# Attention and routing phase of a fused four-block model: another order of TensorE's groups

## Chip, cores and metric

The kernel runs on one core of a Trainium2 chip. The metric is the device time of one execution in microseconds (us), the median of several runs. A profile of one execution, taken apart from those runs, gives the rows shown here.

## What is computed

Four layers, each a cross attention and a feed-forward block, on `x` of 16 x 256 x 256 in float32. Only the first three steps lie in phase A, which the change touches:

```python
x = x + tanh(g_xattn[0]) * _L0_xattn_ref(ctx, _layernorm(x), mask, ...)   # 16 heads of 64, keys: 256 context + 256 latent tokens
x = x + tanh(g_ffn[0]) * _L0_ffn_ref(_layernorm(x), ...)                  # attention over 256 tokens, 16 heads of 16, gated heads
x = x + tanh(g_xattn[1]) * _L1_xattn_ref(_layernorm(x), ctx, W_out, b_out, 16)   # 16 heads of 16, keys = values = context
...
```

In the wide attention (`_L0_xattn_ref`) `sim = q @ k.T`, masked, softmax over 512 keys, times `v`, times `Wout`, layer norm. Phase A also computes the router logits of the next step (an argmax over 32 experts).

## The kernel before

Everything is written by hand for five engines that meet at semaphores. Phase A has one loop over rounds `i = -1 .. B+1` (B = 16). Round `i` works on three batches at once: the wide attention of batch `i`, the narrow attention "f" (the gated one) of batch `f = i-1` with its end, and the narrow attention "c" of batch `c0 = i-2`. A round has eight **pairs** `u` of wide heads, and a pair has five **places** `p = 5u .. 5u+4`; `beside(i, p)` holds the narrow work of a place. Each engine runs the same loop over its own part, in program order.

TensorE's (PE's) groups, with the letters used from here on, the line of the profile and the part of the 128 x 128 array that a matmul of theirs uses (rows*columns as the trace prints it):

| letter | function | line | array | what |
|---|---|---|---|---|
| S | `scores(w,u,t)` | L543 | 64*128 | scores of two wide heads, for query tile t = 0 or 1 |
| K, Q | `keys`, `pair_queries` | L522, L531 | 128*128 | keys, queries of the **next** pair |
| V | `values` | L551 | 128*128 | values of this pair |
| PT | `weights_by_key` | L561 | 128*128 | transposes of softmax weights, four per pair |
| AV | `pair_values` | L573 | 128*64 | weights times values of the pair **before** |
| wo | `wide_out` | L584 | 128*128 | output projection |
| bq, bk | `by_query`, `by_key` | L689, L703 | 32*128 | narrow scores, four groups g = 0..3 each, once by query and once by key |
| vo | `values_out` | L718 | 128*32 | narrow weights times values |
| tq, tt, to, cT | `turn_queries`, `turn_tiles`, `turn_out`, `c_keys` | L666, L612, L731, L658 | 128*128 | transposes |
| fq, fk | `f_rows`, `f_keys` | L625, L633 | 128*128 | narrow projections |
| gate, elog, cnt | `f_gate`, `e_logits`, `e_count` | L641, L747, L219/L220 | 128*128 | gate logits, router logits, expert counts |

"S1" is S for t = 1; "bq3" is bq with g = 3. The part of the array is called the **mode** below.

PSUM is shared by order. The wide work rotates through 3 banks (`w_order`, a list that names every wide group in PE's order): a group may start when the group three places before it in that list has been taken out by its reader. The narrow scores rotate through 2 slots of two banks (`n_order`), and one bq or bk fills both. Readers: VectorE (DVE) masks each S (`mask_scores`, L1080, one per head), reduces each half of a bq to its maxima (`maxima`, L1155), and copies half of the PTs (L1090). ScalarE (ACT) copies K, Q, V and AV (L884, L889, L894, L901), takes the exponentials of the wide weights in SBUF (`exps`, L877) and of each half of a bk out of PSUM (L934), and copies the transposed queries of a tq (L924), which the next bq or bk reads. GpSimd scales the wide weights.

Of the kernel before, what the change touches and what calls it, by code (L numbers as in the profile page):

```python
# [89 lines left out]
PAIRS = HEADS // 2  # L90
# [4 lines left out]
def build(nc, a, out, B, stages):  # L95
# [5 lines left out]
    with top:  # L101
# [130 lines left out]
        def on(b):  # L232
            return 0 <= b < B
# [7 lines left out]
        if "A" in stages:  # L241
            with ExitStack() as ph:
# [58 lines left out]
                def filled(i, p):  # L301

                    return fill.get((i, p), [])

                w_order = []
                for i in range(-1, B + 2):
                    for u in range(PAIRS):
                        nw, nu = pair_after(i, u)
                        bw, bu = pair_before(i, u)
                        w_order += [("S", i, u, 0, j) for j in range(2)] * on(i) + [("K", nw, nu)] * on(nw)  # L310
                        w_order += [("wo", i - 1)] * (u == 1 and on(i - 1)) + filled(i, 5 * u)
                        w_order += [("S", i, u, 1, j) for j in range(2)] * on(i) + [("Q", nw, nu)] * on(nw) + filled(i, 5 * u + 1)
                        w_order += [("V", i, u)] * on(i)
                        w_order += [("lT", i + 1)] * (u == 6 and on(i + 1)) + filled(i, 5 * u + 2)
                        w_order += [("AV", bw, bu)] * on(bw)
# [8 lines left out]
                for i in range(B + 2):  # L324
                    f, c0 = i - 1, i - 2
# [5 lines left out]
                with Stage() as ctx:  # L331
# [168 lines left out]
                    def _(pe):  # L500
# [250 lines left out]
                        def e_count(b):  # L751
                            pe.wait_ge(e_chosen, b + 1)
                            route_count(pe, rb, b, vbank).then_inc(vr.full(("rk", b)), 1)

                        def beside(i, p):
                            f, c0 = i - 1, i - 2
                            if on(c0):
                                if p == 1:
                                    queries_again("c", c0)
                                if 2 <= p <= 5:  # L760
                                    by_key("c", c0, p - 2)
                                if 3 <= p <= 6:
# [8 lines left out]
                                if p == 18:  # L771
                                    e_turn(c0)
                                if p == 20:
                                    e_logits(c0)
                                if p == 23:
                                    e_count(c0)
                            if on(f):
                                if p == 5:
                                    wide_out(f, 0)
                                    wide_out(f, 1)  # L780
                                if p == 11:
                                    f_turn(f)
                                if p == 12:
                                    f_rows(("fq", f), f, fq)
                                if p == 13:
                                    f_keys(f)
                                if p == 14:
                                    f_rows(("fv", f), f, fv)
# [8 lines left out]
                                if 24 <= p <= 27:  # L797
                                    values_out("f", f, p - 24)
                                if p == 28:
# [11 lines left out]
                                if 36 <= p <= 38:  # L811
                                    by_query("c", f, p - 36)
                            if on(i + 1):
                                if p == 32:
                                    features(("lT", i + 1), i + 1, 0)
                                if p == 33:
                                    features(("xT", i + 1), i + 1, 2)

                        pe.wait_ge(made, 2)
                        for i in range(-1, B + 2):  # L820
# [3 lines left out]
                            for u in range(PAIRS):  # L824
                                nw, nu = pair_after(i, u)
# [2 lines left out]
                                    scores(i, u, 0)  # L828
                                if u == 0 and on(i - 2):
                                    by_query("c", i - 2, 3)  # L830
                                if on(nw):
                                    keys(nw, nu)
                                beside(i, 5 * u)
                                shared(i, 5 * u)
                                if on(i):
                                    scores(i, u, 1)
                                if u == 4 and on(i - 1):
                                    by_query("f", i - 1, 3)
                                if on(nw):
                                    pair_queries(nw, nu)  # L840
                                beside(i, 5 * u + 1)
                                shared(i, 5 * u + 1)
                                if on(i):
                                    values(i, u)
                                beside(i, 5 * u + 2)
                                shared(i, 5 * u + 2)
                                if on(bw):
                                    pair_values(bw, bu)
# [12 lines left out]
                    def _(act):  # L861
# [150 lines left out]
                        for i in range(-1, B + 2):  # L1012
                            for u in range(PAIRS):
                                nw, nu = pair_after(i, u)
                                bw, bu = pair_before(i, u)
                                if on(nw):
# [4 lines left out]
                                shared_tanh(i, 5 * u)  # L1021
                                if on(nw):
                                    pair_queries(nw, nu)
                                if u == 3 and on(i - 1):
                                    turn_queries(("f", "Q", i - 1))
                                if on(i):
                                    exps(i, u, 1)
                                beside(i, 5 * u + 1)
                                shared_tanh(i, 5 * u + 1)
                                if on(i):  # L1030
                                    values(i, u)
                                beside(i, 5 * u + 2)
                                shared_tanh(i, 5 * u + 2)
                                if on(bw):
                                    pair_values(bw, bu)
# [13 lines left out]
                    def _(dve):  # L1049
# [167 lines left out]
                        def beside(i, p):  # L1217
# [6 lines left out]
                                if p == 9:  # L1224
                                    c_add(c0)
                            if on(f):
                                if p == 5:
                                    wide_take(f)
                                if p == 7:
                                    wide_ask(f)  # L1230
# [1644 lines left out]
```

## Time and profile before

| what | value |
|---|---|
| median of 3 runs | 4381.85 us (4377.96 to 4382.2) |
| the profiled execution: its own time | 4407.42 us |
| its span from first to last instruction | 4405.7 us |
| PE busy | 4046.3 us, 92% of the span |
| DVE, ACT, GpSimd busy | 53%, 40%, 21% |
| one steady round of phase A | 146.90 us |

Phase A is the first 2300 us or so of the span. PE is the engine to read: it is busy nearly all the time there, and its idle time has a releaser beside it, the engine whose work ended the wait. In the timeline a row is a run of equal instructions; the difference between the starts of two rows of PE is what the first one costs, waits included. The "us" column of a matmul row is a modelled end and overlaps the next row.

### The profile page before, as it was taken

The page shows a single profiled execution, that of the slowest core. Times are in us where ns is not written, and L with a number is a line of the kernel's source. Part 1 is how long each engine was busy: PE and PEld are TensorE (multiplying, and loading weights), DVE is VectorE, ACT ScalarE, POOL GpSimd, SP SyncE. Part 2 cuts the span into 40 slices and gives each one's busy share as a digit, 9 for nine tenths or more (in the row PEclk, how much of TensorE's full clock was granted, in tenths as well). Part 3 has the DMA queues.
Part 4 walks back from the last instruction along what each step waited for, and adds up shares of the span by engine and source line. Part 5 has one row for each costly group of instructions (what it writes and reads, how often), then busy time and mean ns, then how long its engine had stood idle before and what let it go on. Part 6 is the DMA issues. An engine that isn't in the chain of part 4 may idle for free. (4 is left out here: it accounts for less than half of the span.)

```text
span 4405.7 us, 78115 instructions
## 1 busy us (share of the span) xinstructions
PE 4046.3 (92%) x29168; PEld 2823.8 (64%) x29168; DVE 2319.0 (53%) x7158; ACT 1776.4 (40%) x3733; POOL 945.1 (21%) x1115
## 2 busy tenths in 40 slices
PE   7999999999999999999999899988899998679986
PEld 4666666666666666666665599956666665448853
DVE  4555655565556555655554422135666665474434
ACT  4445544554455445554542111112444444213310
POOL 2221222122212221222120011110111100015556
PEclk9999999999999999999999999999999999889998
DMA  3000000000000000000000289920100100029944
GB/s 112 3 3 6 8 8 4 6 8 8 4 6 8 8 4 6 8 7 5 4 30 15 77 284 332 335 92 13 34 20 20 32 18 13 17 96 326 325 143 131
DMA packets 136623, 284.25 MB, mean 65 GB/s; under 512 B 19968, under 2 KB 90176, under 8 KB 127680
## 3 DMA queue, kind: packets, MB, share of 16 engines
q1 hardware_dynamic: 84944, 200.03, 13.2%
q0 software_dynamic: 18336, 50.09, 3.8%
q10 hardware_dynamic: 32976, 29.13, 1.9%
q8 instruction: 243, 3.98, 0.4%
q14 instruction: 124, 1.02, 0.1%
HBM read 229.12 MB, written 50.07 MB: 63 GB/s over the span
## 5 line engine op out<-in xcount | busy, mean ns | idle before, releaser
L459 POOL TENSOR_SCALAR a_wide_p<-a_wide_p,a_w_inv 128x512 f32<-128x512 f32 x512 | 354.8, 705 | 1427.0 <-DVE a_w_inv L1085 1427.0
L877 ACT ACTIVATE a_wide_p<-a_wide_p,a_row_min 128x512 f32<-128x512 f32 x512 | 363.5, 713 | 6.1 <-DVE a_row_min L1080 2.8
L1080 DVE CUSTOM_DVE_ANT_0 a_wide_p<-ring,a_neg_keys 128x512 f32<-128x512 f32 x434 | 285.1, 688 | 124.5 <-PE ring L543 124.2
L1155 DVE TENSOR_REDUCE a_q_pad<-ring 128x4 f32<-128x1024 f32 x256 | 301.4, 1220 | 90.0 <-PE ring L689 88.1
L543 PE MATMUL ring<-a_qk 64*128 64x512 f32 x868 | 288.5, 640 | 19.7 <-DVE a_wide_pt L1090 15.5
L934 ACT ACTIVATE a_probs<-ring 128x1024 f32<-128x1024 f32 x256 | 250.5, 1018 | 76.4 <-PE ring L703 76.4
L1574 PE MATMUL ring<-b_xgt,b_we 128*128 128x128 f32 x2016 | 235.5, 275 | 0.5 <-DVE b_xgt L1737 0.5
L1574 PEld LDWEIGHTS ring<-b_xgt,b_we 128*128 128x128 f32 x2016 | 230.2, 192 | 0.8 <-DVE b_xgt L1737 0.7
L2640 DVE CUSTOM_DVE_ANT_0 c_junk<-ring,c_neg_mask 128x256 f32<-128x256 f32 x512 | 181.4, 420 | 90.0 <-PE ring L2170 90.0
L573 PE MATMUL ring<-a_wide_pt,a_v 128*64 128x256 f32 x1792 | 219.5, 387 | 0.0
L551 PEld LDWEIGHTS ring<-shared_w,a_kv_t 128*128 128x128 f32 x1568 | 185.0, 192 | 20.0 <-issue 12.3
L551 PE MATMUL ring<-shared_w,a_kv_t 128*128 128x128 f32 x1568 | 195.6, 278 | 1.7
L1503 POOL DMA_INDIRECT d_xg<-d_rows,d_token_idx x159 | 150.3, 945 | 183.9 <-PE ring L1563 82.7
L884 ACT ACTIVATE a_qk<-acc 128x512 f32<-128x512 f32 x82 | 49.0, 597 | 310.5 <-PE acc L522 310.5
L689 PE MATMUL ring<-a_k_t,a_q_t 32*128 32x256 f32 x2048 | 146.6, 399 | 27.7 <-DVE a_q_pad L1155 22.6
L573 PEld LDWEIGHTS ring<-a_wide_pt,a_v 128*64 128x64 f32 x1792 | 119.3, 137 | 81.2 <-issue 21.2
L703 PE MATMUL ring<-a_q_t,a_k_t 32*128 32x256 f32 x2048 | 147.6, 401 | 23.5 <-ACT a_probs L934 18.2
L561 PE MATMUL ring<-ident,a_wide_p 128*128 128x128 f32 x1208 | 164.0, 275 | 5.5 <-ACT a_kv_t L868 4.9
L1747 DVE TENSOR_TENSOR b_hid<-b_sil,ring 128x512 f32<-128x512 f32 x63 | 43.3, 687 | 238.2 <-ACT b_sil L1635 238.2
L1574 PE MATMUL ring<-d_xgt,d_we 128*128 128x128 f32 x1272 | 168.2, 275 | 0.5 <-DVE d_xgt L1737 0.5
L522 PE MATMUL acc<-a_kv_t,shared_w 128*128 128x512 f32 x328 | 164.4, 624 | 1.2 <-ACT a_kv_t L868 1.2
L2441 ACT ACTIVATE c_probs<-ring 128x1024 f32<-128x1024 f32 x128 | 125.7, 1023 | 94.9 <-PE ring L2186 94.9
(461 smaller groups left out, 8421.8 us busy)
## 6 DMA issues: line engine op xcount, KB each, us to landing
b_we<-in_experts SPq DMA_DIRECT2D x63, 1536.0 KB
d_we<-in_experts SPq DMA_DIRECT2D x159, 256.0 KB
d_results<-d_yb ACTq DMA_DIRECT2D x159, 128.0 KB
b_results<-b_yb ACTq DMA_DIRECT2D x63, 128.0 KB
a_cb<-in_ctx SPq DMA_DIRECT2D x16, 256.0 KB, 2.8
b_turned<-a_heads_t SPq DMA_DIRECT2D x16, 256.0 KB
b_rows<-a_heads SPq DMA_DIRECT2D x16, 256.0 KB
shared_x<-b_turned SPq DMA_DIRECT2D x8, 512.0 KB, 5.4
```

Of the source, the lines that this page charges most:

```text
L459: ins = pool.tensor_scalar(wide_p[:, h % 4, t, :], wide_p[:, h % 4, t, :], w_inv[:, t, h:h + 1], 1.0, ALU.mult, ALU.mult)
L522: ins = pe.matmul(wbank(name), wkv[:, c, u * P:(u + 1) * P], kv_t[w % 2][:, c, :], start=(c == 0), stop=(c == C - 1))
L543: pe.matmul(wbank(name), qk[u % 2][64 * j:64 * j + 64, t * P:(t + 1) * P], qk[u % 2][64 * j:64 * j + 64, 256:768], start=True, stop=True). ...
L551: ins = pe.matmul(wbank(name)[:, P * i:P * i + P], kv_t[w % 2][:, c, i * P:(i + 1) * P], wkv[:, c, 1024 + u * P:1024 + (u + 1) * P], start ...
L561: ins = pe.transpose(wbank(name)[:, P * k:P * k + P], wide_p[:, (2 * u + h) % 4, t, k * P:(k + 1) * P], ident[:])
L573: ins = pe.matmul(wbank(name)[64 * h:64 * h + 64, 0:256], v4[u % 2][:, k, 64 * h:64 * h + 64], wide_pt[:, h, k, :], start=(k == 0), stop=( ...
L877: ins = act.activation(wide_p[:, h % 4, t, :], wide_p[:, h % 4, t, :], ACT.Exp, scale=-1.0, bias=row_min[:, h, t:t + 1], accum_out=row_sum ...
L934: act.activation(probs[:, i % 4, :, :, :].rearrange("p j k n -> p (j k n)"), nslot(name), ACT.Exp, scale=HD ** -0.5 if k == "c" else 1.0). ...
L1080: dve.tensor_tensor_reduce(wide_p[:, h % 4, t, :], wbank(name), neg_keys[w % 2][:], -0.125, 3.0e38, ALU.add, ALU.min, row_min[:, h, t:t + ...
L1155: dve.tensor_reduce(q_pad[:, :, 2 * i:2 * i + 2, HD].rearrange("p t h -> p h t"), s, AX.X, ALU.max, negate=True).then_inc(nr.taken(name), 1)
L1574: ins = pe.matmul(ring[:, rg.slot(("gu", u)), UP * j + P * i:UP * j + P * i + P], we[:, u % WB, w0:w0 + P], xgt[:, u % 2, c, :], start=(c ...
L2640: ins = dve.tensor_tensor_reduce(junk[:, 4 * (i % 2) + 2 * j + t, :], s[:, j, t, :], neg_mask[:, t, :], -1.0, 3.0e38, ALU.add, ALU.min, q_ ...
```

## The change

It rearranges PE's groups within a pair and moves no work to another engine. Two tables of pair numbers decide it. In the pairs of `late` (0, 1, 4, 5) K of the next pair stands behind S1 in place of in front of it. In the pairs of `near` (1, 2, 5, 6) AV of the pair before stands right behind S1, and Q and V come after it. `w_order` (the rotation) and ACT's program follow the same tables. Single groups move too: bq3 of "f" goes ahead of S1 in pair 4, bq0 of "c" goes ahead of Q in pair 7, wo from place 5 to 6, elog from place 20 to 19, two of the vo stand together at place 27. DVE's program changes in two places: `maxima("f", f, 3)` moves from place 21 to 20, and `wide_take` from 5 to 6. No instruction is added or dropped.

```diff
+                late = (0, 1, 4, 5)
+                near = (1, 2, 5, 6)
...
-                                if p == 20:
+                                if p == 19:
                                     e_logits(c0)
...
-                                if p == 5:
+                                if p == 6:
                                     wide_out(f, 0)
...
-                                if on(nw):
+                                if u == 4 and on(i - 1):
+                                    by_query("f", i - 1, 3)
+                                if u not in late and on(nw):
                                     keys(nw, nu)
                                 beside(i, 5 * u)
                                 shared(i, 5 * u)
                                 if on(i):
                                     scores(i, u, 1)
-                                if u == 4 and on(i - 1):
-                                    by_query("f", i - 1, 3)
+                                if u in near:
+                                    if on(bw):
+                                        pair_values(bw, bu)
+                                    beside(i, 5 * u + 1)
+                                    shared(i, 5 * u + 1)
+                                if u == PAIRS - 1 and on(i - 1):
+                                    by_query("c", i - 1, 0)
+                                if u in late and on(nw):
+                                    keys(nw, nu)
                                 if on(nw):
                                     pair_queries(nw, nu)
...
-                                if p == 21:
+                                if p == 20:
                                     maxima("f", f, 3)
```

**PE, pairs 3 and 4 of a steady round**, from the second bq on. Before (rows of S1 and of the PTs that name `ring` or `acc` are the same group in another bank):

```order
L689 MATMUL ring<-a_k_t,a_q_t 128x256 x8
L561 MATMUL acc<-ident,a_wide_p 128x128 x4
...
L689 MATMUL ring<-a_k_t,a_q_t 128x256 x8
L543 MATMUL ring<-a_qk 128x512 x2
L522 MATMUL acc<-a_kv_t,shared_w 128x512 x2
L747 MATMUL acc<-b_route_w,a_heads_t 128x32 x4
L543 MATMUL ring<-a_qk 128x512 x2
L689 MATMUL ring<-a_k_t,a_q_t 128x256 x8
L531 MATMUL acc<-a_kv_t,shared_x 128x256 x2
```

After, the same stretch (lines are 7 higher):

```order
L696 MATMUL ring<-a_k_t,a_q_t 128x256 x8
L619 MATMUL acc<-ident,a_heads 128x128 x4
L568 MATMUL acc<-ident,a_wide_p 128x128 x4
...
L754 MATMUL acc<-b_route_w,a_heads_t 128x32 x4
L696 MATMUL ring<-a_k_t,a_q_t 128x256 x8
L550 MATMUL ring<-a_qk 128x512 x2
L696 MATMUL ring<-a_k_t,a_q_t 128x256 x8
L550 MATMUL acc<-a_qk 128x512
L550 MATMUL ring<-a_qk 128x512
L529 MATMUL ring<-a_kv_t,shared_w 128x512 x2
L538 MATMUL acc<-a_kv_t,shared_x 128x256 x2
```

Between bq2 and bq3 there stood S, K, elog and S1; now S alone stands there, and elog is ahead of bq2.

**DVE at the same place**: before, the masks of S and S1 stand together around the router logits, and the maxima of bq3 follow.

```order
L1155 TENSOR_REDUCE a_q_pad<-ring 128x2x2 x2
L1080 ISA a_wide_p,a_row_min<-ring,a_neg_keys 128x512
L1080 ISA a_row_min 128x1
L1080 ISA a_wide_p,a_row_min<-ring,a_neg_keys 128x512
L1080 ISA a_row_min 128x1
L186 COPY b_logits<-acc 128x64
L1080 ISA a_wide_p,a_row_min<-ring,a_neg_keys 128x512
...
L1155 TENSOR_REDUCE a_q_pad<-ring 128x2x2 x2
```

After:

```order
L1198 TENSOR_REDUCE a_q_pad<-ring 128x2x2 x2
L1123 ISA a_wide_p,a_row_min<-ring,a_neg_keys 128x512
L1123 ISA a_row_min 128x1
L1123 ISA a_wide_p,a_row_min<-ring,a_neg_keys 128x512
L1123 ISA a_row_min 128x1
L1198 TENSOR_REDUCE a_q_pad<-ring 128x2x2 x2
L186 COPY b_logits<-acc 128x64
L1123 ISA a_wide_p,a_row_min<-acc,a_neg_keys 128x512
```

The maxima of bq3 have moved ahead of the mask of S1.

The whole round as letters, read from the two orders, with | where the mode changes and - where it stays:

```
before                                              after
0 S|bq|K|S|Q-tq-V|bk|AV|bk|vo|PT4|bk|vo|            S|bq|S|K-Q-tq-V|bk|AV|bk|vo|PT4|bk|vo|
1 S|K|bk|vo|wo|S|Q|vo|V-to|AV|tt-PT4-proj|          S|bk|vo|S|AV|vo|wo-K-Q-to-V-tt-PT4-proj|
2 S|K|S|Q-tt-V-fq|AV|fk-PT4-fv|                     S|K|S|AV|tt-Q-fq-V-fk-PT4-fv|
3 S|K|S|Q-tq-V|bq|AV|tt|bq|PT4|bq|                  S|K|S|Q-tq-V|bq|AV|bq|tt-PT4-elog|bq|
4 S|K-elog|S|bq|Q-V-tq|AV|cnt|bk|PT4|bk|vo|         S|bq|S|K-Q-V-tq|AV|bk|cnt-PT4|bk|vo|
5 S|K|bk|vo|S|Q|bk|vo|V|vo|AV|to-PT4-tt|            S|bk|vo|S|AV|bk|K-Q|vo-vo|V-to-PT4-tt|
6 S|K-gate|S|Q-proj-V-cT-lT|AV|xT-PT4|              S|K-gate|S|AV|proj-Q-cT-lT-V-xT-PT4|
7 S|K-tq|S|Q|bq|V|bq|AV|PT2|bq|PT2|                 S|K-tq|S|bq|Q-V|bq|AV|PT2|bq|PT2|
```

Over all of phase A the mode changes 1270 times in PE's order before and 1048 times after; in a steady round (2 to 14) 78 and 64 times, counting the change to the next round's S.

## Rows read from the trace of the kernel before

**Rows 1.** Windows, a steady round: us, busy PE, PEld, DVE, ACT, POOL, clock, DMA share, GB/s

```profile
983.90:1130.80 146.90, 141.61 (x1078) 94.22 (x1078) 84.55 (x231) 75.36 (x158) 32.61 (x40) 1.00 0.02 7
```

**Rows 2.** Timeline, PE: the four PT of pair 3, two of them in the second row

```profile
1059.70 0.66 PE L561 MATMUL acc<-ident,a_wide_p 128*128 128x128 f32 x4
1060.20 1.04 PE L561 MATMUL ring<-ident,a_wide_p 128*128 128x128 f32 x8
1061.07 0.63 PE L561 MATMUL acc<-ident,a_wide_p 128*128 128x128 f32 x4
```

**Rows 3.** Timeline, PE: one K and two V, each with the row that follows it

```profile
1029.07 1.98 PE L522 MATMUL acc<-a_kv_t,shared_w 128*128 128x512 f32 x4
1030.99 1.13 PE L543 MATMUL ring<-a_qk 64*128 64x512 f32 x4
...
1018.14 2.05 PE L551 MATMUL ring<-shared_w,a_kv_t 128*128 128x128 f32 x16
1020.02 1.04 PE L731 MATMUL ring<-ident,a_o_t 128*128 128x128 f32 x8
...
1106.10 1.95 PE L551 MATMUL ring<-shared_w,a_kv_t 128*128 128x128 f32 x16
1107.88 1.04 PE L658 MATMUL ring<-ident,a_v_pad 128*128 128x128 f32 x8
```

**Rows 4.** Timeline, PE, pairs 3 and 4, from bq1 to bk0

```profile
1058.63 1.15 PE L689 MATMUL ring<-a_k_t,a_q_t 32*128 32x256 f32 x16
...
1062.30 1.15 PE L689 MATMUL ring<-a_k_t,a_q_t 32*128 32x256 f32 x16 [0.60 <-DVE a_q_pad L1155]
1063.38 1.13 PE L543 MATMUL ring<-a_qk 64*128 64x512 f32 x4
1064.44 1.98 PE L522 MATMUL acc<-a_kv_t,shared_w 128*128 128x512 f32 x4
1066.26 0.97 PE L747 MATMUL acc<-b_route_w,a_heads_t 128*128 128x32 f32 x8
1067.19 1.13 PE L543 MATMUL ring<-a_qk 64*128 64x512 f32 x4
1068.25 1.15 PE L689 MATMUL ring<-a_k_t,a_q_t 32*128 32x256 f32 x16
...
1073.32 1.95 PE L573 MATMUL ring<-a_wide_pt,a_v 128*64 128x256 f32 x16
1075.20 0.19 PE L219 MATMUL acc<-b_pairs,earlier 128*128 128x32 bf16 x1
...
1075.39 1.15 PE L703 MATMUL ring<-a_q_t,a_k_t 32*128 32x256 f32 x16
```

**Rows 5.** Timeline, DVE: maxima of bq2, then the first mask of S

```profile
1063.47 2.36 DVE L1155 TENSOR_REDUCE a_q_pad<-ring 128x4 f32<-128x1024 f32 x2
1065.74 0.68 DVE L1080 CUSTOM_DVE_ANT_0 a_wide_p<-ring,a_neg_keys 128x512 f32<-128x512 f32 x1
```

**Rows 6.** Timeline, pair 0: DVE's maxima of bq3; PE's Q, tq and bk0

```profile
986.56 2.35 DVE L1155 TENSOR_REDUCE a_q_pad<-ring 128x4 f32<-128x1024 f32 x2
...
989.03 1.13 PE L531 MATMUL ring<-a_kv_t,shared_x 128*128 128x256 f32 x4
990.00 1.04 PE L666 MATMUL ring<-ident,a_q_pad 128*128 128x128 f32 x8
...
993.11 1.15 PE L703 MATMUL ring<-a_q_t,a_k_t 32*128 32x256 f32 x16 [0.29 <-ACT a_q_t L924]
```

**Rows 7.** Timeline, PE: pair 2's S and fq

```profile
1028.02 1.13 PE L543 MATMUL ring<-a_qk 64*128 64x512 f32 x4 [0.93 <-DVE a_wide_pt L1090]
...
1035.81 1.97 PE L625 MATMUL acc<-a_fq,a_x_t 128*128 128x256 f32 x8 [0.41 <-ACT a_x_t L920]
```

**Rows 8.** Timeline, pair 7: PE's Q, bq0 and bq1

```profile
1119.33 1.13 PE L531 MATMUL ring<-a_kv_t,shared_x 128*128 128x256 f32 x4
1120.56 1.15 PE L689 MATMUL ring<-a_k_t,a_q_t 32*128 32x256 f32 x16
...
1124.23 1.15 PE L689 MATMUL ring<-a_k_t,a_q_t 32*128 32x256 f32 x16 [0.55 <-DVE a_q_pad L1155]
```

More of the change, by code:

```diff
@@ L309, in build @@
                         bw, bu = pair_before(i, u)
-                        w_order += [("S", i, u, 0, j) for j in range(2)] * on(i) + [("K", nw, nu)] * on(nw)
-                        w_order += [("wo", i - 1)] * (u == 1 and on(i - 1)) + filled(i, 5 * u)
-                        w_order += [("S", i, u, 1, j) for j in range(2)] * on(i) + [("Q", nw, nu)] * on(nw) + filled(i, 5 * u + 1)
+                        w_order += [("S", i, u, 0, j) for j in range(2)] * on(i)
+                        w_order += [("K", nw, nu)] * (u not in late and on(nw)) + filled(i, 5 * u)
+                        w_order += [("S", i, u, 1, j) for j in range(2)] * on(i)
+                        w_order += [("AV", bw, bu)] * (u in near and on(bw))
+                        w_order += ([("wo", i - 1)] * (u == 1 and on(i - 1)) + filled(i, 5 * u + 1)) * (u in near)
+                        w_order += [("K", nw, nu)] * (u in late and on(nw)) + [("Q", nw, nu)] * on(nw)
+                        w_order += filled(i, 5 * u + 1) * (u not in near)
+                        w_order += ([("lT", i + 1)] * (u == 6 and on(i + 1)) + filled(i, 5 * u + 2)) * (u in near)
                         w_order += [("V", i, u)] * on(i)
-                        w_order += [("lT", i + 1)] * (u == 6 and on(i + 1)) + filled(i, 5 * u + 2)
-                        w_order += [("AV", bw, bu)] * on(bw)
+                        w_order += (filled(i, 5 * u + 2) + [("AV", bw, bu)] * on(bw)) * (u not in near)
                         w_order += [("xT", i + 1)] * (u == 6 and on(i + 1)) + filled(i, 5 * u + 3)
@@ L796, in beside @@
                                     by_key("f", f, p - 23)
-                                if 24 <= p <= 27:
+                                if p == 24 or p == 25:
                                     values_out("f", f, p - 24)
+                                if p == 27:
+                                    values_out("f", f, 2)
+                                    values_out("f", f, 3)
                                 if p == 28:
@@ L810, in beside @@
                                     queries("c", f)
-                                if 36 <= p <= 38:
+                                if 37 <= p <= 38:
                                     by_query("c", f, p - 36)
+                            if on(c0):
+                                if p == 18:
+                                    e_turn(c0)
+                                if p == 23:
+                                    e_count(c0)
                             if on(i + 1):
@@ L836, in _ @@
                                     scores(i, u, 1)
-                                if u == 4 and on(i - 1):
-                                    by_query("f", i - 1, 3)
+                                if u in near:
[7 more added lines that the diff above has]
+                                    keys(nw, nu)
                                 if on(nw):
                                     pair_queries(nw, nu)
[L841 to L848, printed above, removed]
+                                if u in near:
+                                    beside(i, 5 * u + 2)
+                                    shared(i, 5 * u + 2)
+                                    if on(i):
+                                        values(i, u)
+                                else:
+                                    beside(i, 5 * u + 1)
+                                    shared(i, 5 * u + 1)
+                                    if on(i):
+                                        values(i, u)
+                                    beside(i, 5 * u + 2)
+                                    shared(i, 5 * u + 2)
+                                    if on(bw):
+                                        pair_values(bw, bu)
                                 if u == PAIRS - 1 and on(i):
@@ L1015, in _ @@
                                 bw, bu = pair_before(i, u)
-                                if on(nw):
+                                if u not in late and on(nw):
                                     keys(nw, nu)
@@ L1021, in _ @@
                                 shared_tanh(i, 5 * u)
+                                if u in near:
+                                    if on(i):
+                                        exps(i, u, 1)
+                                    if u > 1 and on(bw):
+                                        pair_values(bw, bu)
+                                    beside(i, 5 * u + 1)
+                                    if u == 1 and on(bw):
+                                        pair_values(bw, bu)
+                                    shared_tanh(i, 5 * u + 1)
@@ L1022, in _ @@
+                                if u in late and on(nw):
+                                    keys(nw, nu)
                                 if on(nw):
                                     pair_queries(nw, nu)
[L1024 to L1035, printed above, removed]
+                                if u in near:
+                                    beside(i, 5 * u + 2)
+                                    shared_tanh(i, 5 * u + 2)
+                                    if on(i):
+                                        values(i, u)
+                                else:
+                                    if u == 3 and on(i - 1):
+                                        turn_queries(("f", "Q", i - 1))
+                                    if on(i):
+                                        exps(i, u, 1)
+                                    beside(i, 5 * u + 1)
+                                    shared_tanh(i, 5 * u + 1)
+                                    if on(i):
+                                        values(i, u)
+                                    beside(i, 5 * u + 2)
+                                    shared_tanh(i, 5 * u + 2)
+                                    if on(bw):
+                                        pair_values(bw, bu)
@@ L1226, in beside @@
                             if on(f):
-                                if p == 5:
+                                if p == 6:
                                     wide_take(f)
```

4 lines of the change are left out of this document (removed).

## The prediction

> **What bounds the kernel now.** I read the windows first, then the timeline of PE over one steady round, then DVE's and ACT's timeline beside its waits. A steady round takes 146.90 us and PE is busy for 141.61 of them, so PE idles 5.29; the granted clock is 1.00, the 2.4 GHz level, and plays no part; DVE (84.55) and ACT (75.36) have room on average [rows 1]. What counts is therefore PE's own cost per group, and the few places where the next group waits for a reader: narrow scores that wait for maxima (0.60 and 0.55 us), a bk that waits for ACT's copy of the turned queries (0.29), S of pair 2 behind a long DVE stretch (0.93), fq behind ACT (0.41) [rows 4, 6 to 8].
>
> **Price of a mode change.** Two parts show in start-to-start times. Leaving: K followed by S, another mode, takes 1.92 us; K followed by elog, the same mode, takes 1.82 [rows 3, 4]. The rows round 0.09 or so up and down, and I count 0.093. Entering: V behind vo takes 1.88, V behind a group of its own mode 1.78, both left without a change [rows 3]: 0.10 more. For K and Q, which in the kernel before always come from another mode, I take V's 0.10, because they load full weights just as V does; nothing shows them without it. Nothing shows 64*128 followed by 128*64 (S then AV) either; I take 0.09, a change like any other, and keep 0 and 0.2 as its ends, which is 4 places a round and +-0.4 us.
>
> The Trainium skill's page "TensorEngine Tiling (Array Packing)", Key Properties, says that a change of the tiling mode, not of the tile alone, drains the engine. The 0.09 us on leaving agree with it, and by that rule alone the change could only gain: 222 changes at 0.093 are 20.6 us, 4361.
>
> **What the removed changes are worth.** The order has 14 fewer changes in a steady round: 14 x 0.093 = 1.30 us. Groups that newly come from their own mode: Q in pairs 0, 1, 2, 4, 5, 6, K in pair 1, V in pairs 1 and 7, fk in pair 2; proj in pair 6 newly comes from another. Net 9 x 0.10 = 0.94, and a net 0.22 for four transposing groups, which cost 0.50 as the first after a change and 0.44 otherwise [rows 2]. Together **2.46 us a round** if no wait changes. V in pair 7 is in this sum.
>
> **What the new order makes wait.** I walked the round with the durations of the rows, each group starting at the later of PE's turn and the release of what it needs. From the rows: bq, bk 1.08 (1062.30 to 1063.38), S 1.06, elog 0.93 [rows 4]; Q 0.97, and 0.87 from its own mode; tq 0.87 before its own mode [rows 6]; V 1.78 [rows 3]; AV 1.88 (1073.32 to 1075.20) [rows 4]; PT 0.44 [rows 2].
>
> *Pairs 3 and 4* carry most of it. bq2 starts at 1062.30 and its maxima at 1063.47, 2.36 us for both halves [rows 4, 5]. bq3 fills the same two slots, so it can't start before bq2 + 1.17 + 2.36 + 0.15 = bq2 + 3.68. Before, S, K, elog and S1 (4.87 us) cover that, and bq3 starts 5.95 after bq2 [rows 4]. Now only S does. bq1 stays at 1058.63 (it waits for DVE in both); behind it come tt 0.49, four PT 1.75, 0.18 for the last PT (its bank is emptied by ACT, which now has the copy of tt first) and elog 0.93, so bq2 starts at 1063.06 in place of 1062.30. S ends 2.14 later, at 1065.20, and bq3 waits until 1066.74: **a new wait of 1.54 us**. S1 follows at 1067.81, K at 1068.87 and ends at 1070.69. Q needs the bank of S1's first half. DVE masks it late, because the maxima of bq3 now come first: 1066.74 + 1.17 + 2.3 for the maxima, 0.3 for the logits (my guess, for a small copy that waits for its own semaphore), 0.68 for the mask [rows 5], 0.1 to PE: 1071.28, **another wait of 0.6**. Then Q 0.87, V 1.78, tq 0.97, AV 1.88: bk0 at 1076.78 against 1075.39. After bk0 both orders hang on the same ACT exponentials. Net +1.40, the removed changes already inside.
>
> *Pair 0.* bq3 of "c" starts as before and its maxima begin at 986.56, 2.35 long [rows 6]. S1 now stands right behind bq3, but DVE reaches its mask only at 988.84, so Q, three places behind S1's first half, can start at 989.6 and not at 989.03. ACT then copies Q (0.1 earlier after its start, since Q is shorter), takes the exponentials of S1 and copies tq, in this order; so the copy ends 0.45 later, and bk0 moves from 993.11 to 993.56 [rows 6]. Net +0.46.
>
> *Pair 7.* bq0 of "c" now stands ahead of Q. In the old order Q is in front of it and bq0 still waits 0.17 (1119.33 to 1120.56, Q being 1.06) for ACT's copy of tq. That copy doesn't come earlier, so PE now waits from 1119.33 to 1120.56, does bq0, Q and V (1.08 + 0.97 + 1.88) and has bq1 at 1124.49 against 1124.23; the old wait of 0.55 there is gone [rows 8]. Net +0.26.
>
> *Pairs that gain.* Pair 1: five fewer changes bring the group `to` 0.37 earlier. DVE's stretch from there (divide heads, layer norm, both copies of PT) sets S of pair 2 at 1028.02 [rows 7], so it moves with it: -0.37. Pair 2: fq waits for ACT's copy of tt, which now stands behind the exponentials of S1 and the copy of AV, 0.3 later than before (1035.81 [rows 7]); what V and fk save just covers it: -0.09. Pair 5: -0.47 by changes, +0.2 for a bk and a vo that wait for ACT: -0.27. Pair 6: ACT's `features` set its end in both: -0.09.
>
> **Sum.** 1.40 + 0.46 + 0.26 - 0.37 - 0.09 - 0.27 - 0.09 = **+1.3 us a round**, the waits growing by 3.76 us and the changes giving 2.46. Rounds 2 to 14 are alike: 13 x 1.3 = +17. Rounds 0 and 1: with no narrow work between, S1 stands directly behind S in six pairs and waits 0.9 for the mask of S, three places before its second half; against that, pair 1 of round 1 has wo ahead of its long wait and gains 2. Together about 0. The last round and the tail: +0.5. Other phases aren't touched. **+17 us**: against the profiled execution's own 4407.42 it is 4424; that execution lies 25.6 above the median of the runs, and the median goes from 4381.85 to **4399**.
>
> **Rivals.** (a) *The waits only move and don't grow*: the changes' 2.46 us a round, with 222 x 0.093 = 20.6 on leaving and 17.7 on entering in all of phase A, come off whole: 4381.85 - 38 = 4344. For it: PE is the busiest engine, and DVE and ACT have over 60 us of slack a round [rows 1]. Against it: that slack isn't at bq3. A milder form ends on the faster side too: the wait ahead of bq3 in pair 4 is overlapped, because bq3 in fact starts when DVE has finished one half. It decides from a growth of waits under 2.46 a round; with bq3's 1.54 and half of the other losses away, the sum is -0.8 x 14 = -11: 4371. (b) *Even*: my +1.3 is a difference of 3.76 and 2.46, and 0.6 less leaves it within 8.8 us of before. This happens if entering costs K and Q more than V's 0.10, or if DVE gets to S1's masks 0.3 sooner at pairs 0 and 4: 4381 to 4390. (c) *Worse*: waits behind ACT's new order that I took as covered, above all AV's copy in pair 1, which by the code must wait for the whole of wo and holds ACT for 7 us, or the exponentials of S1 in pair 4, reach PE: another 1 us a round, 4413.
>
> The skill's same page, PSUM Bottleneck, says that row tiling speeds the matmuls up but not the emptying of PSUM. The rows agree: 1.08 us on PE fill what takes DVE 2.36 [rows 4, 5]. It speaks for my forecast: groups of one mode side by side bring narrow scores closer together than DVE can empty them.
>
> **How the numbers follow.** A measurement of this kernel can tell 0.2% (8.8 us) from nothing. Slower as forecast, (c) with it: 0.62. Even: 0.19. Faster, whole or mild: 0.19. The range takes in (c) at the top (4418) and the milder form of (a) at the bottom (4366), and leaves the full gain out.
>
> **What would show it.** In the changed kernel's round: length 148.2 us and idle time of PE near 9 us in place of 5.3; mode changes cheaper by Q at 0.87 behind K; a wait of 1.5 us at bq of pair 4 released by the maxima, one of 0.6 at Q of pairs 4 and 0 released by the mask, one of 1.2 at bq0 of pair 7 released by ACT; the 0.60 at bq2 of pair 3 and the 0.55 at bq1 of pair 7 gone; S of pair 2 still behind DVE, now for 1.3 us. Wrong if the wait at bq3 is under 0.5 us, or if the round is under 146.

## The result and the profile after

| | before | after |
|---|---|---|
| median of 5 runs each | 4381.85 us | 4400.27 us (4395.28 to 4414.67) |
| ratio | | 1.0048, 95% interval 1.0037 to 1.0060 |
| a steady round | 146.90 us | 148.05 us |

The change makes the kernel 18.4 us slower. A ratio here and below, with its interval, is estimated from the executions of both kernels; it isn't the quotient of the two medians, which is 1.0042 here. The profiled executions took 4407.42 and 4414.67 us, both longer than any of the other executions of their kernel, and their spans (4405.7 and 4412.9 us) differ by less than the medians, so I compare rounds. In the page of after, PE is busy for less time than the 4046.3 us of before, and yet the kernel is slower:

```profile
span 4412.9 us, 78115 instructions
PE 4023.8 (91%) x29168; PEld 2835.4 (64%) x29168; DVE 2329.2 (53%) x7158; ACT 1770.5 (40%) x3733; POOL 946.1 (21%) x1115
```

The same steady round by windows (columns as in [rows 1]):

```profile
990.20:1138.25 148.05, 139.75 (x1076) 94.42 (x1077) 84.89 (x231) 74.76 (x158) 32.62 (x40) 1.00 0.02 6
```

Against [rows 1] PE's busy time fell by 1.86 us and its idle time rose from 5.29 to 8.30, by 3.01; the difference is the 1.15 us by which the round grew. (The idle time beside a row is less than the real wait, since the end of a matmul row is modelled; where sizes matter below, they are taken from starts.) The clock is 1.00, the 2.4 GHz level, as before. The view of PE's waits in this round says who is waited for (total, times, longest):

```profile
PE ring L696 <- DVE a_q_pad L1198: 2.2, 2, 1.5
PE ring L696 <- ACT a_q_t L950: 1.2, 1, 1.2
PE ring L550 <- DVE a_wide_pt L1133: 1.1, 1, 1.1
...
PE acc L632 <- ACT a_x_t L946: 0.6, 1, 0.6
PE ring L538 <- DVE a_row_min L1123: 0.3, 1, 0.3
...
PE acc L538 <- DVE a_row_min L1123: 0.3, 1, 0.3
```

Before, all the bq waited 1.1 us in the round for their maxima, and no Q for a mask. PE's timeline shows the places. Pairs 3 and 4 (compare [rows 4]), from bq1 to Q:

```profile
1065.05 1.15 PE L696 MATMUL ring<-a_k_t,a_q_t 32*128 32x256 f32 x16 [0.73 <-DVE a_q_pad L1198]
...
1068.45 0.98 PE L754 MATMUL acc<-b_route_w,a_heads_t 128*128 128x32 f32 x8
1069.36 1.15 PE L696 MATMUL ring<-a_k_t,a_q_t 32*128 32x256 f32 x16
1070.43 1.13 PE L550 MATMUL ring<-a_qk 64*128 64x512 f32 x4
1073.04 1.15 PE L696 MATMUL ring<-a_k_t,a_q_t 32*128 32x256 f32 x16 [1.48 <-DVE a_q_pad L1198]
...
1075.17 1.98 PE L529 MATMUL ring<-a_kv_t,shared_w 128*128 128x512 f32 x4
1077.49 1.13 PE L538 MATMUL acc<-a_kv_t,shared_x 128*128 128x256 f32 x4 [0.33 <-DVE a_row_min L1123]
```

bq3 stands one S behind bq2 and waits. DVE's timeline at that place (compare [rows 5]) shows for what, and why Q waits too, three groups after bq3:

```profile
1070.54 2.36 DVE L1198 TENSOR_REDUCE a_q_pad<-ring 128x4 f32<-128x1024 f32 x2 [0.77 <-PE ring L696]
1072.81 0.68 DVE L1123 CUSTOM_DVE_ANT_0 a_wide_p<-ring,a_neg_keys 128x512 f32<-128x512 f32 x1
...
1074.21 2.36 DVE L1198 TENSOR_REDUCE a_q_pad<-ring 128x4 f32<-128x1024 f32 x2
1076.48 0.21 DVE L186 COPY b_logits<-acc 128x64 f32<-128x64 f32 x1
1076.73 0.69 DVE L1123 CUSTOM_DVE_ANT_0 a_wide_p<-acc,a_neg_keys 128x512 f32<-128x512 f32 x1
```

The maxima of bq2 end at 1072.90 and bq3 starts at 1073.04. The mask of S1's first head ends at 1077.42 behind the maxima of bq3, and Q starts at 1077.49.

The other places in PE's timeline (compare [rows 6 to 8]): pair 0's Q and bk0, S of pair 2, fq, and bq0, Q, V, bq1 of pair 7:

```profile
995.90 1.13 PE L538 MATMUL ring<-a_kv_t,shared_x 128*128 128x256 f32 x4 [0.35 <-DVE a_row_min L1123]
...
999.91 1.15 PE L710 MATMUL ring<-a_q_t,a_k_t 32*128 32x256 f32 x16 [0.22 <-ACT a_q_t L950]
...
1034.44 1.13 PE L550 MATMUL ring<-a_qk 64*128 64x512 f32 x4 [1.12 <-DVE a_wide_pt L1133]
...
1042.50 1.97 PE L632 MATMUL acc<-a_fq,a_x_t 128*128 128x256 f32 x8 [0.63 <-ACT a_x_t L946]
...
1127.78 1.15 PE L696 MATMUL ring<-a_k_t,a_q_t 32*128 32x256 f32 x16 [1.16 <-ACT a_q_t L950]
1128.86 1.13 PE L538 MATMUL ring<-a_kv_t,shared_x 128*128 128x256 f32 x4
1129.82 1.95 PE L558 MATMUL acc<-shared_w,a_kv_t 128*128 128x128 f32 x16
1131.70 1.15 PE L696 MATMUL ring<-a_k_t,a_q_t 32*128 32x256 f32 x16
```

The distances between the first S of successive pairs, taken from the timelines of both traces, give what each pair cost (us, after less before):

| pair | forecast | measured |
|---|---|---|
| 0 | +0.46 | +0.47 |
| 1 | -0.37 | -0.37 |
| 2 | -0.09 | -0.02 |
| 3 and 4 | +1.40 | +1.28 |
| 5 | -0.27 | -0.37 |
| 6 | -0.09 | -0.09 |
| 7 | +0.26 | +0.25 |
| round | +1.3 | +1.15 |

### The profile page after: what moved, and what is told of

It is laid out like the page before. It is cut to its first block and busy times, and to the rows that moved or that the text cites. A ratio compares the mean times of both kernels' runs of the same rounds, so it can differ in the third digit from the quotient of the medians.

```text
span 4412.9 us, 78115 instructions
## 1 busy us (share of the span) xinstructions
PE 4023.8 (91%) x29168; PEld 2835.4 (64%) x29168; DVE 2329.2 (53%) x7158; ACT 1770.5 (40%) x3733; POOL 946.1 (21%) x1115
## 5 line engine op out<-in xcount | busy, mean ns | idle before, releaser
L1123 DVE CUSTOM_DVE_ANT_0 a_wide_p<-ring,a_neg_keys 128x512 f32<-128x512 f32 x387 | 256.1, 687 | 100.3 <-PE ring L550 99.9
L580 PE MATMUL ring<-a_wide_pt,a_v 128*64 128x256 f32 x1520 | 186.7, 388 | 0.0
L696 PEld LDWEIGHTS ring<-a_k_t,a_q_t 32*128 32x128 f32 x2048 | 95.9, 184 | 113.4 <-issue 108.0
L558 PE MATMUL ring<-shared_w,a_kv_t 128*128 128x128 f32 x1328 | 164.8, 277 | 1.7
L558 PEld LDWEIGHTS ring<-shared_w,a_kv_t 128*128 128x128 f32 x1328 | 157.5, 192 | 13.5 <-issue 6.5
L1133 DVE COPY a_wide_pt<-acc 128x512 f32<-128x512 f32 x127 | 87.5, 689 | 129.8 <-PE acc L568 129.8
```

What stands on the lines that cost most here:

```text
L558: ins = pe.matmul(wbank(name)[:, P * i:P * i + P], kv_t[w % 2][:, c, i * P:(i + 1) * P], wkv[:, c, 1024 + u * P:1024 + (u + 1) * P], start ...
L580: ins = pe.matmul(wbank(name)[64 * h:64 * h + 64, 0:256], v4[u % 2][:, k, 64 * h:64 * h + 64], wide_pt[:, h, k, :], start=(k == 0), stop=( ...
L696: ins = pe.matmul(nslot(name)[:, n:n + 256], q_t[SLOT * r:SLOT * r + SLOT, g, t * P:(t + 1) * P], k_t[SLOT * r:SLOT * r + SLOT, g, :], sta ...
L1123: dve.tensor_tensor_reduce(wide_p[:, h % 4, t, :], wbank(name), neg_keys[w % 2][:], -0.125, 3.0e38, ALU.add, ALU.min, row_min[:, h, t:t + ...
```

## The experiments

**The theory, called "local waits" below.** Each pair's entry in the table hangs on its own edit, so edits can be undone one by one and their rounds add up; what is lost in pairs 3 and 4 is DVE's time to empty the narrow scores. The rivals are named in each expectation. What follows phase A is the same program in all kernels and yet takes 1892 to 1939 us in the twelve traces, so the round decides where times don't. A "ratio" is against the kernel before on the same chip. The first four kernels ran on one chip, where the kernel before took 4383.85 us.

**1. Pairs 3 and 4 put back.** After, with

```diff
-                late = (0, 1, 4, 5)
+                late = (0, 1, 5)
...
-                                if u == 4 and on(i - 1):
-                                    by_query("f", i - 1, 3)
...
+                                if u == 4 and on(i - 1):
+                                    by_query("f", i - 1, 3)
...
-                                if p == 20:
+                                if p == 21:
```

The second pair of lines stands behind S1; the last is `maxima("f", f, 3)`; tt, elog and cnt are back too.

> The changed kernel with pairs 3 and 4 as before: K ahead of S1 in pair 4, bq3 behind S1, elog and cnt at their old places, the maxima of bq3 at place 21. Local waits (my theory): the round of 148.05 us loses the 1.28 us that pairs 3 and 4 gained, so 146.8, and the median comes back to that of before within 0.1% (4382). Rival, the loss is spread over the round by ACT's new order and the changed rotation: less than half of it comes back, round above 147.4, median 4390 or more.

Windows of its steady round:

```profile
983.40:1130.20 146.80, 140.11 (x1076) 94.66 (x1077) 84.39 (x231) 74.87 (x158) 32.62 (x40) 1.00 0.02 6
```

The round is 146.80, 1.25 under the 148.05 of after; the median is 4382.36, ratio 1.0006 (0.9996 to 1.0016). These two pairs are worth more than the whole loss of 1.15 a round.

**2. Pairs 3 and 4 alone.** Before, with only the edits that kernel 1 takes back (and `late = (4,)`, `near = ()`).

> The kernel before with the new pairs 3 and 4 alone. Local waits: round 146.90 + 1.28 = 148.2 us, median 4400, though 3 mode changes a round fewer. Rival, loss spread over the round: under half of that, round 147.5 or less, median under 4391.

Windows of its steady round:

```profile
991.20:1139.40 148.20, 141.28 (x1076) 94.05 (x1077) 85.08 (x231) 75.22 (x158) 32.60 (x40) 1.00 0.02 6
```

PE's timeline, bq3 and Q of pair 4:

```profile
1073.99 1.15 PE L696 MATMUL ring<-a_k_t,a_q_t 32*128 32x256 f32 x16 [1.48 <-DVE a_q_pad L1193]
...
1078.43 1.13 PE L538 MATMUL acc<-a_kv_t,shared_x 128*128 128x256 f32 x4 [0.33 <-DVE a_row_min L1118]
```

The round is 148.20, +1.30 (+1.28 by the starts of S); the two waits are the same to the hundredth. The median is 4405.91 us, ratio 1.0066 (1.0047 to 1.0085): this one edit alone, which has 3 mode changes a round fewer, makes the kernel at least as slow as the whole change.

**3. S1's mask ahead of the maxima of bq3.** After, with one number changed on DVE, so that the second wait should go and the first stay:

```diff
-                                if p == 20:
+                                if p == 21:
                                     maxima("f", f, 3)
```

> The changed kernel with one line of DVE's program back: the maxima of bq3 behind the mask of S1 in pair 4 (place 21). Local waits: the wait of Q for that mask (0.33 us shown as idle, about 0.5 in start times) goes, tq doesn't begin to wait, round 147.5, 7 us less than the changed kernel: 4393. Rival, the wait only moves to tq or to the ACT chain behind bk0: round 148.0, no difference to the changed kernel.

Windows of its steady round:

```profile
988.60:1136.10 147.50, 139.50 (x1076) 94.57 (x1077) 84.42 (x231) 74.77 (x158) 32.62 (x40) 1.00 0.02 6
```

PE's timeline, K and Q of pair 4, 1.82 apart with no wait between them; bq3 ahead of them still waits 1.48:

```profile
1073.61 1.98 PE L529 MATMUL ring<-a_kv_t,shared_w 128*128 128x512 f32 x4
1075.43 1.03 PE L538 MATMUL acc<-a_kv_t,shared_x 128*128 128x256 f32 x4
```

The round is 147.50, 0.55 less, as forecast. The time is inconclusive: 4400.71 us, ratio 1.0042 (1.0026 to 1.0058), an interval that holds after's 1.0048 and also the 1.003 that the round gives (14 x 0.55 = 8 us less). The trace shows one thing that works against the gain: behind the steady rounds, where there is no S1 to mask, tq of the last "f" waits 1.59 us for the maxima, which DVE now takes behind its work on the shared groups; in after it doesn't wait. So the order of DVE's two readers accounts for 0.55 of the 1.28 us. The rest belongs to the other parts of the edit; the wait of 1.48 at bq3 is the largest of them, but no kernel moves bq3 by itself.

**4. Only the pairs that gain.** Kernel 1, with pairs 0 and 7 put back too (`late = (1, 5)`, bq0 of "c" behind Q).

> Only the pairs that gained keep the new order (1, 2, 5, 6); pairs 0, 3, 4 and 7 stand as before. Local waits: round 146.90 - 0.37 - 0.02 - 0.37 - 0.09 = 146.05 us, 14 rounds and a little at the start: 12 us less than the kernel before, 4370. Rival, the losses belong to the changed ACT order of the near pairs as well: round not under 146.9, median 4380 or more.

Windows of its steady round:

```profile
981.40:1127.40 146.00, 140.21 (x1076) 94.55 (x1077) 84.43 (x231) 74.93 (x158) 32.71 (x40) 1.00 0.02 7
```

The round is 146.05 by the starts of S (the window above is cut at tenths), 0.85 less than before; the median is 4369.71 us, ratio 0.9975 (0.9963 to 0.9987). With 9 mode changes a round fewer, the gain is real where no wait takes it, and this version beats both kernels.

The next four ran on another chip, where the kernel before took 4414.35 us; their times are compared with that.

**5. elog as cover of bq2, bq3 back behind S1.** Kernel 4, with tt, elog and cnt at after's places: the one part of the edit of pairs 3 and 4 that brings no scores closer together.

> As the kernel with the gaining pairs only, but pair 3 keeps the new order (tt behind bq1, elog at 19 ahead of bq2) and cnt its new place behind bk0; K stays ahead of S1 and bq3 behind S1 in pair 4, maxima of bq3 at 21. Local waits: elog and tt fill PE's wait for the maxima of bq1, and S, K and S1 (4.0 us) still cover the 3.68 us between bq2 and bq3, so no new wait: round 146.05 - 0.6 = 145.4 us, median about 4361. Rival, the wait moves on to bq3 or to tq of pair 4, which needs the maxima of bq3: round 146.0.

PE's timeline, from bq2:

```profile
1059.37 1.15 PE L696 MATMUL ring<-a_k_t,a_q_t 32*128 32x256 f32 x16
1060.45 1.13 PE L550 MATMUL ring<-a_qk 64*128 64x512 f32 x4
1061.51 1.99 PE L529 MATMUL acc<-a_kv_t,shared_w 128*128 128x512 f32 x4
1064.27 1.13 PE L550 MATMUL ring<-a_qk 64*128 64x512 f32 x4 [0.78 <-DVE a_row_min L1121]
```

DVE's timeline, maxima of bq2 and the first mask of S:

```profile
1060.55 2.36 DVE L1196 TENSOR_REDUCE a_q_pad<-ring 128x4 f32<-128x1024 f32 x2 [0.77 <-PE ring L696]
1062.82 0.68 DVE L1121 CUSTOM_DVE_ANT_0 a_wide_p<-ring,a_neg_keys 128x512 f32<-128x512 f32 x1
```

The round is 146.5, neither 145.4 nor the rival's 146.0: both missed. elog had also stood between K and S1, and without it S1 waits 0.78 us for the mask of S, which DVE reaches only behind the maxima of bq2. The saved wait ahead of bq2 came back three groups further on as another. The median is 4405.66 us, ratio 0.9987 (0.9975 to 0.9999).

**6. DVE's copies of PT earlier in its long stretch ahead of pair 2.** Kernel 5, with half of the layer norm moved behind the copies, so that S of pair 2 is freed earlier:

```diff
+                                if p == 9:
+                                    wide_give(f)
+                                    norm_ask(f_norm, "f", lambda t: xb(f, t))
...
-                                if p == 8:
-                                    wide_give(f)
-                                    norm_ask(f_norm, "f", lambda t: xb(f, t))
```

> The last one, and in pair 1 DVE copies the transposed weights before the second half of the layer norm (wide_give and the statistics at place 9, ahead of the addition of c). It takes away the 1.1 us for which S of pair 2 waits. If that wait is DVE's order alone: round 0.7 us shorter, 144.7, median about 4352, with some 0.4 us back at S1 of pair 2. Rival, DVE is late in total there and the mask of S comes as much later: round within 0.2 of the last one.

PE's timeline, pair 2:

```profile
1026.42 1.13 PE L550 MATMUL ring<-a_qk 64*128 64x512 f32 x4
1027.48 1.98 PE L529 MATMUL acc<-a_kv_t,shared_w 128*128 128x512 f32 x4
1030.61 1.13 PE L550 MATMUL ring<-a_qk 64*128 64x512 f32 x4 [1.14 <-DVE a_row_min L1121]
```

S starts 1.19 earlier in the round and waits for nothing, but now S1 waits 1.14 for the mask of S, and pair 3 begins at the same 62.48 us of the round. The round is 146.5 again. Here the rival was right: the amount of DVE's work ahead of S1 is the bound there and not its order. The median is 4416.71 us, ratio 1.0005 (0.9993 to 1.0017), 11 us above kernel 5 with the same round. By the traces 2.6 of these lie ahead of the steady rounds and 4.0 behind them; the rest lies outside phase A.

**7 and 8. Pair 0 alone, pair 7 alone.** Before, with `late = (0,)`; and before, with bq0 of "c" ahead of Q. One execution each, so only the rounds are read.

> The kernel before with the new pair 0 alone (K behind S1). Local waits: round 146.90 + 0.47 = 147.4 us, with one mode change less. Rival, pair 0 loses only beside the other changed pairs: 146.8 or less.

PE's timeline, Q and bk0 of kernel 7:

```profile
991.40 1.13 PE L538 MATMUL ring<-a_kv_t,shared_x 128*128 128x256 f32 x4 [0.35 <-DVE a_row_min L1117]
...
995.41 1.15 PE L710 MATMUL ring<-a_q_t,a_k_t 32*128 32x256 f32 x16 [0.22 <-ACT a_q_t L944]
```

> The kernel before with the new pair 7 alone (bq0 ahead of Q). Local waits: round 146.90 + 0.25 = 147.15 us, bq0 waiting 1.16 us for ACT and bq1 not at all. Rival: the wait of bq0 and the saved mode change cancel, 146.9 or less.

PE's timeline, bq0 and bq1 of kernel 8:

```profile
1123.65 1.15 PE L696 MATMUL ring<-a_k_t,a_q_t 32*128 32x256 f32 x16 [1.16 <-ACT a_q_t L946]
...
1127.57 1.15 PE L696 MATMUL ring<-a_k_t,a_q_t 32*128 32x256 f32 x16
```

The rounds are 147.40 and 147.16: +0.49 and +0.25, with the same waits as in after. With kernels 2 and 4 the parts add up, by the starts of S: 1.28 + 0.49 + 0.25 - 0.86 = +1.16 against 1.15 measured.

**9 and 10. Half the maxima.** Before and after, each with the maxima taken over the first 128 of the 256 keys, so that DVE empties a bq faster; this leaves out half of the maximum's inputs. The kernel before took 4384.16 us on that chip.

```diff
-dve.tensor_reduce(q_pad[:, :, 2 * i:2 * i + 2, HD].rearrange("p t h -> p h t"), s, AX.X,
+dve.tensor_reduce(q_pad[:, :, 2 * i:2 * i + 2, HD].rearrange("p t h -> p h t"), s[:, :, :, 0:128], AX.X,
```

> The kernel before with every maxima of phase A taken over the first 128 of 256 keys, so the stabiliser of the narrow softmax is another one, and DVE needs about half of the 2.36 us for a pair of halves. PE's order is untouched. The waits for the maxima in pairs 3, 4 and 7 (0.27, 0.69, 0.26, 0.72 us in start times) go: round about 145.0 us in place of 146.90.

Windows of kernel 9, then its group of maxima in that round:

```profile
972.60:1117.60 145.00, 141.09 (x1078) 93.96 (x1078) 76.19 (x231) 75.27 (x158) 32.63 (x40) 1.00 0.02 7
```

```profile
L1155 DVE TENSOR_REDUCE a_q_pad<-ring 128x4 f32<-128x512 f32 x16 | 10.3, 685 | 7.0 <-PE ring L689 7.0
```

> The same cut in the changed kernel. If the changed order loses by the time that DVE takes to empty the narrow scores, its waits at bq1, bq3 and Q of pair 4 and Q of pair 0 shrink by some 2.7 us, and the two kernels come together: round 145.3, only 0.3 above the other one with the same cut (1.15 without it). Rival, the loss hangs on ACT's order or on the rotation of the banks alone: the difference stays at 1.0 or more.

Windows of kernel 10:

```profile
971.10:1115.80 144.70, 138.96 (x1078) 94.55 (x1078) 76.58 (x231) 74.77 (x158) 32.62 (x40) 1.00 0.02 7
```

Kernel 10: PE's timeline from bq2 to the bq3 of pair 4, then DVE's maxima of that bq2:

```profile
1048.61 1.15 PE L696 MATMUL ring<-a_k_t,a_q_t 32*128 32x256 f32 x16
1049.69 1.13 PE L550 MATMUL ring<-a_qk 64*128 64x512 f32 x4
1051.23 1.15 PE L696 MATMUL ring<-a_k_t,a_q_t 32*128 32x256 f32 x16 [0.41 <-DVE a_q_pad L1198]
```

```profile
1049.79 1.29 DVE L1198 TENSOR_REDUCE a_q_pad<-ring 128x4 f32<-128x512 f32 x2 [1.20 <-PE ring L696]
```

With maxima of 0.69 us in place of 1.22 the rounds are 145.0 and 144.7: the same change now makes the round 0.3 us shorter, where with whole maxima it makes it 1.15 longer. The pair of maxima takes 1.29 us in place of 2.36, and bq3 starts 2.62 behind bq2 in place of 3.68: 1.07 and 1.06 us less. bq3's wait fell from 1.48 to 0.41. By pairs, the change costs nothing (-0.02) in pairs 3 and 4 of these kernels, and pair 0 gains 0.26; pair 7, whose bq0 waits for ACT, loses 0.86, and pairs 1, 2, 5 and 6 gain as before. I had forecast +0.3 for the change, so the size was missed, and with it the sign. The times point the same way: 4346.1 us (ratio 0.9906, 0.9882 to 0.9931) and 4335.91 us (0.9890, 0.9868 to 0.9911). That kernel 9 falls by 38 us where 14 rounds of 1.9 give 27 has its main reason inside phase A, which is 33.0 us shorter by the traces: 5.1 more come off behind the steady rounds, where no wide work covers the maxima, and 0.9 ahead of them.

## Why the prediction was right, and where it was off

**Mode changes.** Leaving: 0.09 as counted. The open price, S then AV, was taken as 0.09 with 0 and 0.2 as ends; in the trace of after S costs 1.06 ahead of AV, as ahead of anything else. Entering: V's 0.10 was carried over to K and Q, and it holds. Behind a group of its own mode K takes 1.72 (1.82 otherwise) and Q 0.86 (0.97). The even case (b) hung on this, or on masks 0.3 us earlier at pairs 0 and 4; there Q waits 0.52 and 0.50 by starts, against 0.6, so it fell. One slip: 9 x 0.10 is 0.90 and not 0.94, so the prediction's own terms add up to 2.42 and not 2.46; that changes nothing in the +1.3, which comes from the pairs. (In the section on the change, the counts 78 and 64 leave out the change to the next round's S; with it they are 79 and 65, and the 14 stays.)

**Pairs 3 and 4: the decisive step, right to 0.12 us.** bq3 starts 3.68 us behind bq2, as worked out; it starts 1.55 later than S alone would let it, forecast 1.54 (the row's 1.48 is less, since the end of S is a modelled one). Q waits 0.50 by starts, forecast 0.6. What was off: I gave the last PT 0.18 for its bank, and bq1 to bq2 took 4.31 in place of 4.43. Kernels 1 and 2 showed that the edit alone costs 1.25 to 1.30, kernel 3 that the Q wait comes from the order of DVE's readers, and kernel 10 that the distance from bq2 to bq3 shrinks with the reader's time.

**Pairs 0 and 7** were right, by place, releaser and size, and kernels 7 and 8 gave them alone. The old waits at bq2 of pair 3 and bq1 of pair 7 are gone, as forecast: another wait ahead of each (0.73 at bq1 of pair 3, which tt no longer covers, and 1.16 at bq0 of pair 7) takes their place.

**Pairs that gain.** Pair 5 gained 0.10 more than forecast, pair 2 0.07 less: S waits 1.12 (forecast 1.3), fq 0.63.

**The sum.** If the changes gave the 2.46 us that the prediction counts, the waits grew by 1.15 + 2.46 = 3.6 us, forecast 3.76; no run gives either of the two for the whole round by itself. Over rounds 0 to 14 the start of round 15 moved by 15.6 us (2159.53 to 2175.09), of which steady rounds make 13 x 1.15 = 15.0, forecast 17. Rounds 0 and 1, forecast as 0 together, took 1.5 longer: round 0 grew by 1.7 and round 1 shrank by 0.2. In after the first S of all starts 0.8 earlier (24.03 against 24.86; in the twelve traces it lies between 23.9 and 26.1), which hides about half of that. S1 directly behind S in round 0 does wait for the mask:

```profile
26.13 1.13 PE L550 MATMUL ring<-a_qk 64*128 64x512 f32 x4 [0.97 <-DVE a_row_min L1123]
```

The prediction has round 1 gain 2 by having wo ahead of its long wait. That wait, at S of pair 2, did fall from 2.58 to 0.68, but new waits ahead of it took most of the gain.

**Mis-sized: the last round and the tail.** I said +0.5. PE's last group of phase A starts 18.8 us later than before (2500.93 against 2482.16; phase A reaches further than the "2300 us or so" above), so round 15 and the tail cost 3.2. That is 2.7 more than forecast, the largest single error, and the traces show where it sits. In the round behind the last wide batch there is no S, and bq3 of "f" stands right behind bq2:

```profile
2389.99 1.15 PE L696 MATMUL ring<-a_k_t,a_q_t 32*128 32x256 f32 x16
2393.67 1.15 PE L696 MATMUL ring<-a_k_t,a_q_t 32*128 32x256 f32 x16 [2.54 <-DVE a_q_pad L1198]
```

From bq1 to tq this stretch takes 14.20 us against 11.34 before: 2.9 of the 3.2. Before, elog and a piece of the shared work stood between the two, and bq3 did not wait. So the tail holds the same mechanism as pair 4, with nothing left to cover it; kernels 2 and 3 have the same wait of 2.54 there and kernel 1, with the old order, has none. The prediction walked the steady round and put this term at 0.5 without walking the tail.

So the +17 stands for a term of the steady rounds that was 2 us too high and two others that were 1.5 and 2.7 too low. The direction and the mechanism were right; that the median came out within 1.3 us of the 4399 is in part luck.

**Rivals.** (a), that the waits only move, is refuted by after's own idle time (3.01 more) and by kernels 1 and 2; its premise that DVE has 60 us of slack is true and of no use, since DVE is waited for while a bq is emptied. Its milder form, that bq3 starts when DVE has finished one half, is refuted by the rows: bq3 starts at 1073.04, behind the end of both halves at 1072.90. (c) fell: AV's copy behind wo in pair 1 and the exponentials of S1 in pair 4 reached no group of PE. Kernels 9 and 10 show the mechanism itself: the change's sign hangs on how long DVE takes to empty a bq.

The Trainium skill's page "TensorEngine Tiling (Array Packing)", PSUM Bottleneck, says that tiling speeds up TensorE but not the emptying of PSUM. It was the rule that spoke against the change, and the traces agree: 1.08 us of PE's row-tiled work needs 2.36 us of DVE, and two such groups stand 3.68 us apart, with S between them in pair 4 and with nothing between them in the tail.

## What to carry to other kernels

When groups are brought together to save mode changes (0.09 us on leaving, 0.10 more on entering for groups that load full weights), walk the new order with the readers in it: two groups that filled the same PSUM slots here never stood closer than the first's matmuls plus its reader's time (3.68 us, and 2.62 with the shorter maxima), whatever slack that reader had on average. Walk the first and last rounds too, where the work that covers a wait may be missing. A removed filler may have covered two waits, one on each side of it (kernel 5), and moving the reader's work earlier may only hand the wait to the next group (kernel 6). Take such an edit apart by pairs and keep those that gain: here that gave 0.9975 of the time before, where the whole change gave 1.0048.

## What the runs showed of the hardware that was not expected

- Chips differ by 0.7% on the same kernel: the median is 4383.85 and 4384.16 us on two of them, 4414.35 on a third. No kernel was traced on two chips, but the rounds of kernels 7 and 8 came out as the traces of other chips let expect, and what follows phase A did not: 1923 to 1939 us in the four traces of the third chip (kernels 5 to 8), 1892 to 1906 in the six of the other two. A time means something only beside a run of the kernel before on the same chip.
- The maxima take 1.22 us over 1024 values a partition and 0.69 over 512. A line through these two points, an estimate, has 1.05 ns a value and 0.15 us fixed.
- S costs 1.06 us ahead of 128*128, 32*128 and 128*64 groups alike, where nothing waits: which of these modes follows makes no difference.
